# Exponentials and sums first in the next attention slot, and the low halves of the expert weights on DVE instead of POOL

## The chip, the core and the metric

The kernel runs on one core of a Trainium2 chip. The metric is the device time of one launch in microseconds (us). Five engines work side by side, each through its own list of instructions in the order in which they are written: TensorE (PE), VectorE (DVE), ScalarE (ACT), GpSimd (POOL) and SyncE (SP), which here only issues DMAs. They meet through semaphores: `then_inc` counts one up when an instruction has finished, `wait_ge` holds an engine until a count is reached. A wait holds back everything behind it on its engine.

## The reference, cut to what matters

Token selection, one attention layer with quantized values, and a mixture of experts. The part that the change touches first is the softmax in whole numbers, once per batch and head:

```python
x_int = x / scale
x_int = x_int - jnp.max(x_int, axis=-1, keepdims=True)
x_int = jnp.maximum(x_int, n * x0_int)
q = jnp.floor(x_int / x0_int)
r = x_int - x0_int * q
z = r * (r + b_int) + c_int
exp_int = jnp.maximum(jnp.floor(z * jnp.exp2(n - q)), 0.0)
exp_sum = jnp.sum(exp_int, axis=-1, keepdims=True)
ratio = jnp.round(exp_sum / jnp.maximum(exp_int, 1.0))
# out = a power of two that the ratio picks
```

The experts' weights w1 (16 x 192 x 384) and w2 (16 x 192 x 192) meet activations of which the reference takes 32-bit products:

```python
h = jnp.einsum('th,ehf->tef', t, w1) + b1
h = _swiglu(h)
y = jnp.einsum('tei,eih->teh', h, w2) + b2
```

## The kernel before, in words

**Stages.** From 0 to about 74 us tokens are ranked and gathered. From 74 to about 410 us runs attention; from about 429 to 620 us the experts' steps; then the sums are put together. The change lies in the attention.

**Slots.** The 32 batches of 88 tokens are packed in 8 quads of 4 batches, a quad in 3 tiles of 128 rows, which gives 24 tiles. Attention is a software pipeline: `slot(st, n, q)` is written once for each engine, and slot `st` does the softmax of tile `st` and, beside it, work of tiles before and after it. `i = st % 3` is the place in the quad `q = st // 3`. What each engine does in a slot, and in which order, is the order of the calls in its `slot`; nothing is planned at run time.

**The softmax in a slot.** PE makes scores, ACT turns them into whole numbers `S_u` (L934). DVE: maximum `negmx` (L1422), `S_w` (L1427). ACT: the quotient `S_g` (L1011). DVE: remainder `S_rho` (L1461) and the power of two `S_pow` (L1464). ACT: `S_sq`, the square (L1039). DVE: the exponentials `S_e` (L1497) and their sums `esum` (L1501). ACT: an inverse root of `S_e` (L1051) and its square (L1057), both written into `S_sq`; together they are 1/e, called y below. In the next slot DVE makes `S_ratio` (L1446), `S_rb` (L1451) and `S_p` (L1455). SP transposes `S_p` by DMA into `pTs` (`turn_p`, L547), PE multiplies it with the values (`pO`, L1856).

**What else shares the slots.** ACT and PE make the next quad's queries and keys through one PSUM bank `pX`: `project_qk` on PE (L1710), `quant_qk` on ACT (L926). In the slot with i = 0 the chunk 0 comes last, in the one with i = 1 the chunk 5; on PE both stand behind the `pO` matmuls, so behind the transposed `S_p`. Rows of a quad finished two quads ago go to the router: `high_rows` (ACT, i = 0), `low_tail` (DVE, i = 1, L342 and L343), then SP transposes them (`turn_by_load`, L523) ahead of this slot's `S_p`, PE makes the router's logits (`gate_rows`, L1780) and DVE picks four experts per row (`top_experts`, L1350 to L1362). That is in slots 7, 10, 13, 16, 19 and 22, called gate slots below. POOL casts, and sends rows with indirect DMAs (L765).

**Expert weights.** SP loads them in pairs of experts in two staging buffers. A weight is kept as two 16-bit numbers, high and low. ACT scales the pair in place (`scale_pair`, L903 and L905, in the slot with i = 2) and rounds it to the high half (`split_pair`, L912, in the next slot with i = 0, ahead of `S_sq`). POOL subtracts: `low_pair` (L664), 4 instructions per pair, in the slot with i = 0. SP's load of the pair after next waits for these (`stage_low`).

Of the kernel before, what the change touches and what calls it, by code (L numbers as in the profile page):

```python
# [62 lines left out]
def audio_tower(nc, x, tok_w, tok_b, w_qkv, b_qkv, w_proj, b_proj, sw_qkv, sw_proj, s_a1, s_attn,  # L63
                s_a2, s_a3, ffn_scale, gate_w, gate_b, w1, b1, w2, b2, out):
    ctx = ExitStack()
    with ctx:
# [600 lines left out]

# [181 lines left out]
        def _(act):  # L849
# [48 lines left out]
            def scale_pair(m):  # L898

                st, two = stage_in[m % 2], bass.ds(2 * m, 2)  # L900
                act.wait_ge(stage_loaded[m % 2], 16 * 12 * (m // 2 + 1))
                for h in range(2):
                    act.activation(st[:, :, 384 * h:384 * h + 384], st[:, :, 384 * h:384 * h + 384], ACT.Identity,  # L903
                                   scale=fs[:, h:h + 1]).then_inc(s["stage_scaled"], 1)
                act.activation(st[:, :, 768:1152], st[:, :, 768:1152], ACT.Copy, scale=WS).then_inc(s["stage_scaled"], 1)  # L905

            def split_pair(m):

                st, two = stage_in[m % 2], bass.ds(2 * m, 2)
                act.wait_ge(s["stage_scaled"], m * 3 + 3)  # L910
# [1078 lines left out]
```

## Time and profile before

| | us |
|---|---|
| three runs | 658.2, 658.9, 655.73; median 658.2 |
| the profiled execution, its own time | 656.87 |
| its span, first to last instruction | 655.1 |
| DVE busy in the span | 535.2 |
| ACT busy | 443.7 |
| POOL busy | 402.9 |
| PE busy | 369.4 |

The span is 1.77 us shorter than the execution's own time. The shares of busy time are means over stages with different limits, so the attention stage has to be read by itself: by DVE's list in order of time with the idle time before each instruction, and by the chain of waits.

### The profile page before, as it was taken

The numbers are of one execution on the slowest core, as the hardware profiler recorded it, in microseconds if no ns is written. First come the engines' busy times: TensorE is split into PE (matmuls) and PEld (weight loads), VectorE is DVE, ScalarE is ACT, GpSimd is POOL, SyncE is SP. The second block draws the span as 40 slices with busy tenths as digits, with TensorE's granted clock in tenths as the row PEclk, the third lists the DMA queues.
The fourth block names the chain that finished last, engine by engine and source line by source line (L and its number), as shares of the span: only waits on it lengthen the run. The fifth ranks groups of instructions, "written<-read, shape, count | busy, mean of one in ns | idle before, by whom it ended". The sixth has DMA issues, their size and how long they took to land.

```text
span 655.1 us, 13415 instructions
## 1 busy us (share of the span) xinstructions
PE 369.4 (56%) x3593; PEld 236.0 (36%) x3593; DVE 535.2 (82%) x1380; ACT 443.7 (68%) x782; POOL 402.9 (62%) x450
## 2 busy tenths in 40 slices
PE   0598254072452633534536221278979999999264
PEld 0144112031130311312313111256757777777153
DVE  3688699679898897798998989669769998988566
ACT  0046657478767677677686765376878899998753
POOL 9773433431546487586785885477777777777600
PEclk9999555555555555555555555578989999999679
DMA  8546997786959969743422432466467776682098
GB/s 196 67 64 179 366 279 154 257 250 209 304 124 335 226 205 324 154 102 85 114 53 61 101 73 64 107 147 135 116 142 141 124 136 137 137 143 60 14 390 306
DMA packets 191976, 107.76 MB, mean 164 GB/s; under 512 B 137746, under 2 KB 186011, under 8 KB 191906
## 3 DMA queue, kind: packets, MB, share of 16 engines
q1 hardware_dynamic: 181634, 89.22, 56.2%
q0 software_dynamic: 10272, 17.70, 8.8%
q8 instruction: 33, 0.54, 0.4%
q14 instruction: 37, 0.30, 0.2%
HBM read 23.61 MB, written 60.67 MB: 129 GB/s over the span
## 4 chain that ended last, share of the span: by engine, by line
PE 27%; DVE 23%; SPq 13%; issue 13%; DMA 12%; ACT 8%; POOL 2%; DVEq 0%; POOLq 0%; ACTq 0%
PE pS L1925 8%; DMA pTs<-S_p 5%; PE pP L1925 5%; SPq L523 5%; PE pX L1943 4%; DVE S_e L1497 3%; DVE negmx L1422 3%; PE pO L1943 3%; SPq L611 2%; DMA w2s<-expert_rows 2%; SPq L514 2%; PE pS L1666 2%; DMA arena<-in_x_dram 2%; PE pS L1668 2%; DMA bias_rows_hl<-bias_hl 2%
## 5 line engine op out<-in xcount | busy, mean ns | idle before, releaser
L836 POOL DMA_INDIRECT expert_rows<-stage,dest x118 | 124.0, 1051 | 37.3 <-issue 29.6
L765 POOL DMA_INDIRECT region<-rows,slots x60 | 73.7, 1228 | 23.5 <-issue 16.3
L758 POOL CAST arena<-arena 128x384 bf16<-128x384 int8 x42 | 27.0, 643 | 70.0 <-ACT arena L926 69.3
L1843 PE MATMUL pP<-WpT,oq 128*128 128x192 bf16 x72 | 15.9, 359 | 74.0 <-ACT oq L1025 69.2
L1710 PE MATMUL pX<-arena,WA 128*128 128x384 f16 x86 | 34.9, 509 | 39.1 <-ACT arena L926 28.2
L765 POOL DMA_INDIRECT region<-arena,slots x36 | 45.5, 1265 | 18.4 <-issue 11.2
L926 ACT ACTIVATE arena<-pX,qkB,qkA 128x384 int8<-128x384 f32 x43 | 28.4, 661 | 41.6 <-PE pX L1710 41.6
L664 POOL TENSOR_TENSOR w1s<-stage,w1s 128x768 f16<-128x768 f32 (+1 forms) x16 | 33.8, 2113 | 32.9 <-ACT w2s L912 32.3
L1856 PE MATMUL pO<-pTs,vq 88*32 88x96 bf16 (+1 forms) x576 | 12.5, 238 | 71.5 <-DMA pTs<-S_p 71.3
L1497 DVE SCALAR_TENSOR_TENSOR S_e<-S_sq,kf,S_pow 128x1056 f32<-128x1056 f32 x24 | 38.2, 1591 | 16.7 <-ACT S_sq L1039 16.6
L1011 ACT ACTIVATE S_g<-S_w,kf 128x1056 int16<-128x1056 uint16 x24 | 30.3, 1264 | 27.7 <-DVE S_w L1427 27.7
L1051 ACT ACTIVATE S_sq<-S_e,kf 128x1056 f32<-128x1056 f32 x24 | 28.1, 1171 | 26.0 <-DVE S_e L1497 25.7
L1628 DVE TENSOR_SCALAR arena<-pS 128x512 f32<-128x512 f32 x59 | 40.4, 685 | 4.8 <-PE pS L1925 3.6
L1446 DVE SCALAR_TENSOR_TENSOR S_ratio<-esum,S_sq 128x1056 uint16<-128x1056 f32 x24 | 30.9, 1287 | 9.8 <-ACT S_sq L1057 9.8
L1856 PEld LDWEIGHTS pO<-pTs,vq 88*32 88x32 bf16 x576 | 8.6, 118 | 80.7 <-DMA pTs<-S_p 80.4
L1737 PE MATMUL pS<-arena 32*96 32x88 bf16 (+1 forms) x576 | 33.3, 280 | 5.7 <-ACT S_u L934 4.7
L1843 PEld LDWEIGHTS pP<-WpT,oq 128*128 128x128 bf16 x72 | 7.8, 130 | 78.5 <-ACT oq L1025 71.5
L1943 PE MATMUL pX<-w2s,stage 128*128 x264 | 32.6, 250 | 3.8 <-ACT stage L1086 3.0
L1925 PE MATMUL pS<-arena,w1s 128*128 128x256 f16 x224 | 34.0, 283 | 0.0
L1422 DVE TENSOR_REDUCE negmx<-S_u 128x12 f32<-128x1056 int8 x24 | 29.8, 1243 | 4.7 <-ACT S_u L934 4.7
L1461 DVE SCALAR_TENSOR_TENSOR S_rho<-S_g,kf,S_w 128x1056 int16<-128x1056 int16 x24 | 32.6, 1358 | 1.3 <-ACT S_g L1011 1.3
L1427 DVE SCALAR_TENSOR_TENSOR S_w<-S_u,kf,negmx 128x1056 uint16<-128x1056 int8 x24 | 32.4, 1349 | 0.8
(428 smaller groups left out, 1434.6 us busy)
## 6 DMA issues: line engine op xcount, KB each, us to landing
region<-zrow SPq DMA_DIRECT2D x11, 3200.0 KB, 12.2
w1s<-expert_rows SPq DMA_DIRECT2D x16, 384.0 KB, 8.0
stage<-in_L_ffn_w_dram SPq DMA_DIRECT2D x16, 192.0 KB
stage<-in_L_ffn_w_dram SPq DMA_DIRECT2D x32, 96.0 KB
w2s<-expert_rows SPq DMA_DIRECT2D x8, 384.0 KB, 11.7
arena<-in_x_dram SPq DMA_DIRECT2D x4, 672.0 KB
expert_rows<-stage,dest POOLq DMA_INDIRECT x118
out_dram<-xsel SPq DMA_DIRECT2D x8, 198.0 KB
```

Source lines behind the costliest of these rows:

```text
L523: sp.dma_start(xTr[:, :, 128 * i:128 * i + 128], rows[q % 3][:, i, 0:2 * C], transpose=True).then_inc(s["turned"], 16)
L664: pool.tensor_tensor(ws[rows, kind + 1, two, :], st[rows, :, at:at + width], ws[rows, kind, two, :], ALU.subtract).then_inc(s["stage_low"], 1)
L765: pool.indirect_dma_start(region_rows, bass.IndirectOffsetOnAxis(ap=slots[q % 3][:, i, m:m + 1], axis=0), rows[q % 3][:, i, :].bitcast(I16 ...
L836: pool.indirect_dma_start(y_dram, bass.IndirectOffsetOnAxis(ap=dest[(st - 7) % 8][:, j:j + 1], axis=0), ysb[b][:, j, :], None, bounds_chec ...
L1422: dve.tensor_reduce(negmx[:, :], S_u[:, :, :], AX, ALU.max, negate=True).then_inc(s["max_ready"], 1)
L1461: dve.scalar_tensor_tensor(S_rho[:, :, :], S_g[:, :, :], k(K_X), S_w[:, :, :], ALU.mult, ALU.subtract).then_inc(s["rho_ready"], 1)
L1497: dve.scalar_tensor_tensor(S_e[:, :, :], S_sq[:, :, :], k(K_KK), S_pow[:, :, :].bitcast(BF16), ALU.add, ALU.mult).then_inc(s["e_ready"], 1)
L1628: dve.tensor_scalar(lin[r], hidLC[r], -6.0 * XS * WS, 8.0 * XS * WS, ALU.max, ALU.min).then_inc(s["l_done"], 1)
L1710: ins = pe.matmul(bank[:, 0:384], W[:, 128 * c:128 * c + 128], xT[:, kind, :], start=n == 0, stop=n == 2)
L1737: ins = pe.matmul(pS[rows, j, KEEP * c:KEEP * c + width], qT[r][blk, c, at:at + m], keys, start=True, stop=True)
L1925: ins = pe.matmul(dst, w1s[:, kind, bass.ds(k_, 1), 128 * window:128 * window + 128].rearrange("p o f -> p (o f)"), rhs, start=n == 0, sto ...
L1943: ins = pe.matmul(y_ps(st - 5)[:, j, :], lhs, w2s[:, kind, bass.ds(k_, 1), :].rearrange("p o f -> p (o f)"), start=n == 0, stop=n == 4)
```

## The change

1. `S_e` and `esum` leave the end of slot `st` and come at the beginning of slot `st + 1` on DVE: `S_e`, then the choice of experts of the slot before if that was a gate slot, then `negmx`, then `esum`, then `S_w`.
2. The inverse root and the square that make y leave the end of ACT's slot and come first in the next one. They are written into a new buffer `S_y`, so `S_sq` holds only the square of the remainder.
3. ACT no longer scales a weight pair in place: `high_pair` writes the high half with the scale in the same pass, 3 instructions instead of 5, in the slot with i = 2 behind `S_sq`. For pair 0 it comes behind the first `S_u` instead of ahead of it.
4. `low_pair` goes from POOL to DVE: 4 instructions per pair that scale and subtract in one pass, in the slot with i = 0 behind `S_pow`.

```diff
@@ POOL @@
-            def low_pair(m):
-                pool.wait_ge(s["stage_high"], m * 2 + 2)
...
-                    pool.tensor_tensor(ws[rows, kind + 1, two, :], st[rows, :, at:at + width], ws[rows, kind, two, :],
-                                       ALU.subtract).then_inc(s["stage_low"], 1)
-                if i == 0 and st < NT:
-                    low_pair(q)
@@ ACT @@
+            def high_pair(m):
                 act.wait_ge(stage_loaded[m % 2], 16 * 12 * (m // 2 + 1))
                 for h in range(2):
+                    act.activation(w1s[:, 2 * h, two, :], st[:, :, 384 * h:384 * h + 384], ACT.Identity,
+                                   scale=fs[:, h:h + 1]).then_inc(s["stage_high"], 1)
+                act.activation(w2s[:, 0:4:2, two, :].rearrange("p k e f -> p e k f"),
+                               st[:, :, 768:1152].rearrange("p e (k f) -> p e k f", k=2),
+                               ACT.Copy, scale=WS).then_inc(s["stage_high"], 1)
...
-            scale_pair(0)
             quant_scores(0)
-            split_pair(0)
+            high_pair(0)
...
+                if 1 <= st <= NT:
+                    act.wait_ge(s["e_ready"], n)
...
+                    act.activation(S_y[:, :, :], S_e[:, :, :], ACT.Abs_reciprocal_sqrt,
+                                   bias=k(K_TINY)).then_inc(s["inv_root"], 1)
+                    act.wait_ge(s["inv_root"], n)
+                    act.activation(S_y[:, :, :], S_y[:, :, :], ACT.Square).then_inc(s["y_ready"], 1)
...
-                if i == 2 and st <= 20:
-                    scale_pair(q + 1)
-                if i == 0 and 3 <= st < NT:
-                    split_pair(q)
...
                     act.activation(S_sq[:, :, :], S_rho[:, :, :], ACT.Square, bias=k(K_NB2)).then_inc(s["sq_ready"], 1)
+                if i == 2 and st <= 20:
+                    high_pair(q + 1)
@@ DVE @@
+                if 1 <= st <= NT:
+                    dve.wait_ge(s["sq_ready"], n)
+                    dve.wait_ge(s["pow_ready"], n)
...
+                    dve.scalar_tensor_tensor(S_e[:, :, :], S_sq[:, :, :], k(K_KK), S_pow[:, :, :].bitcast(BF16), ALU.add,
+                                             ALU.mult).then_inc(s["e_ready"], 1)
+                if 0 < st <= NT and quad_at(st - 1, GATE) is not None:
+                    top_experts(quad_at(st - 1, GATE))
                 if st < NT:
...
                     dve.tensor_reduce(negmx[:, :], S_u[:, :, :], AX, ALU.max, negate=True).then_inc(s["max_ready"], 1)
+                if 1 <= st <= NT:
+                    dve.wait_ge(s["e_ready"], n)
+                    dve.wait_ge(s["ratio_ready"], n - 1)
+                    dve.tensor_reduce(esum[:, :], S_e[:, :, :], AX, ALU.add).then_inc(s["sum_ready"], 1)
...
+                if i == 0 and st < NT:
+                    low_pair(q)
...
+            def low_pair(m):
+                dve.wait_ge(s["stage_high"], m * 3 + 3)
+                for rows, kind, ws, at, width, scale in (
+                        (slice(0, 128), 0, w1s, 0, 2 * FF, fs[:, 0:1]), (slice(0, CB), 2, w1s, 384, 2 * FF, fs[0:CB, 1:2]),
+                        (slice(0, 128), 0, w2s, 768, C, WS), (slice(0, CB), 2, w2s, 960, C, WS)):
+                    dve.scalar_tensor_tensor(ws[rows, kind + 1, two, :], st[rows, :, at:at + width], scale,
+                                             ws[rows, kind, two, :], ALU.mult, ALU.subtract).then_inc(s["stage_low"], 1)
```

Three places in the order of the instructions. The first is DVE's list at the end of gate slot 10 and the start of slot 11, before; `arena`, `best`, `keep`, `keyv`, `early` belong to `top_experts`.

```order
L1497 SCALAR_TENSOR_TENSOR S_e<-S_sq,kf,S_pow 128x1056
L1501 TENSOR_REDUCE esum<-S_e 128x12
L1350 COPY arena<-pX 128x48
L1353 MAX best<-arena 128x8 x3
L1355 COPY keep<-best 128x3x4
L1357 MATCH_REPLACE keyv<-keep,arena 128x16 x3
L1360 SCALAR_TENSOR_TENSOR early<-keyv,valid 128x48
L1362 TENSOR_TENSOR arena<-arena,best 128x48
L1422 TENSOR_REDUCE negmx<-S_u 128x12
L1427 SCALAR_TENSOR_TENSOR S_w<-S_u,kf,negmx 128x1056
L1435 TENSOR_TENSOR pr<-pP,pA 128x192
```

The same place on DVE after the change (`S_e` here is L1401, `top_experts` L1326 to L1338, `negmx` L1408, `esum` L1412):

```order
L1401 SCALAR_TENSOR_TENSOR S_e<-S_sq,kf,S_pow 128x1056
L1326 COPY arena<-pX 128x48
L1329 MAX best<-arena 128x8 x3
L1331 COPY keep<-best 128x3x4
L1333 MATCH_REPLACE keyv<-keep,arena 128x16 x3
L1336 SCALAR_TENSOR_TENSOR early<-keyv,valid 128x48
L1338 TENSOR_TENSOR arena<-arena,best 128x48
L1408 TENSOR_REDUCE negmx<-S_u 128x12
L1412 TENSOR_REDUCE esum<-S_e 128x12
L1418 SCALAR_TENSOR_TENSOR S_w<-S_u,kf,negmx 128x1056
L1426 TENSOR_TENSOR pr<-pP,pA 128x192
```

`S_e` stays ahead of `top_experts`, which waits for PE; `esum` moved from ahead of `top_experts` to behind `negmx`.

The second is ACT's list from the last score conversion in slot 0 on, before. `arena<-pX` is `quant_qk` of chunk 0, ACT_TABLE_LOAD brings in the table of the inverse root.

```order
L1039 ACTIVATE S_sq<-S_rho,kf 128x1056
L1051 ACT_TABLE_LOAD
L1051 ACTIVATE S_sq<-S_e,kf 128x1056
L926 ACTIVATE arena<-pX,qkB,qkA 128x384
L1057 ACTIVATE S_sq<-S_sq 128x1056
L1011 ACTIVATE S_g<-S_w,kf 128x1056
```

The same place after the change:

```order
L1021 ACTIVATE S_sq<-S_rho,kf 128x1056
L905 ACTIVATE arena<-pX,qkB,qkA 128x384
L989 ACT_TABLE_LOAD
L989 ACTIVATE S_y<-S_e,kf 128x1056
L992 ACTIVATE S_y<-S_y 128x1056
L997 ACTIVATE S_g<-S_w,kf 128x1056
```

The table load and the inverse root stood ahead of `quant_qk`, and stand behind it now.

The third is ACT's list from the last `S_sq` (slot 23) on, before; `arena<-arena 128x48 x6` are the routers' exponentials (`exp_gates`, L968).

```order
L1039 ACTIVATE S_sq<-S_rho,kf 128x1056
L1051 ACTIVATE S_sq<-S_e,kf 128x1056
L1057 ACTIVATE S_sq<-S_sq 128x1056
L962 ACTIVATE rs<-rs 128x3
L968 ACT_TABLE_LOAD
L968 ACTIVATE arena<-arena 128x48 x6
```

The same place after the change:

```order
L1021 ACTIVATE S_sq<-S_rho,kf 128x1056
L941 ACTIVATE rs<-rs 128x3
L947 ACT_TABLE_LOAD
L947 ACTIVATE arena<-arena 128x48 x6
L989 ACT_TABLE_LOAD
L989 ACTIVATE S_y<-S_e,kf 128x1056
L992 ACTIVATE S_y<-S_y 128x1056
```

The exponentials with their table load stood behind y; they stand ahead of it now, and a second table load has come between.

## Rows read from the trace of the kernel before

**Rows 1.** Page, part 1: busy us, share of the span, instructions

```profile
PE 369.4 (56%) x3593; PEld 236.0 (36%) x3593; DVE 535.2 (82%) x1380; ACT 443.7 (68%) x782; POOL 402.9 (62%) x450
```

**Rows 2.** Busy time by stretch: stretch, length, PE, PEld, DVE, ACT, POOL, clock

```profile
271.00:313.00 42.00, 18.64 (x226) 9.77 (x226) 38.28 (x71) 30.66 (x40) 31.69 (x28) 0.50 0.42 100
```

**Rows 3.** Chain that ended last, gate slot 16: start us, length us, engine, tile, line

```profile
300.70 1.18 SPq L523
...
304.57 5.52 DMA pTs<-S_p
```

**Rows 4.** DVE in order of time, slots 15 and 16: start, length, [idle before <-releaser]

```profile
293.24 2.18 DVE L1497 SCALAR_TENSOR_TENSOR S_e<-S_sq,kf,S_pow 128x1056 f32<-128x1056 f32 x1 [1.07 <-ACT S_sq L1039]
295.45 1.25 DVE L1501 TENSOR_REDUCE esum<-S_e 128x12 f32<-128x1056 f32 x1
296.62 1.24 DVE L1422 TENSOR_REDUCE negmx<-S_u 128x12 f32<-128x1056 int8 x1
297.90 1.32 DVE L1427 SCALAR_TENSOR_TENSOR S_w<-S_u,kf,negmx 128x1056 uint16<-128x1056 int8 x1
...
299.40 0.80 DVE L342 TENSOR_TENSOR arena<-tn,arena 128x192 f16<-128x192 f32 x1
...
311.19 0.21 DVE L1350 COPY arena<-pX 128x48 f32<-128x48 f32 x1 [1.77 <-PE pX L1780]
```

**Rows 5.** ACT in order of time, slots 0 and 1

```profile
81.06 1.28 ACT L1051 ACT_TABLE_LOAD   x1
...
85.88 0.67 ACT L926 ACTIVATE arena<-pX,qkB,qkA 128x384 int8<-128x384 f32 x1 [1.16 <-PE pX L1710]
86.45 1.07 ACT L1057 ACTIVATE S_sq<-S_sq 128x1056 f32<-128x1056 f32 x1
```

**Rows 6.** Chain that ended last, slots 1 to 3

```profile
87.55 1.27 DVE S_ratio L1446
...
89.78 2.65 SPq L547
...
95.37 2.45 SPq L480
...
113.79 9.99 DMA bias_rows_hl<-bias_hl
```

**Rows 7.** ACT in order of time, slot 4

```profile
131.88 0.67 ACT L926 ACTIVATE arena<-pX,qkB,qkA 128x384 int8<-128x384 f32 x1 [7.14 <-PE pX L1710]
```

**Rows 8.** DVE in order of time, slots 4, 5 and 6

```profile
133.56 1.26 DVE L1446 SCALAR_TENSOR_TENSOR S_ratio<-esum,S_sq 128x1056 uint16<-128x1056 f32 x1 [5.95 <-ACT S_sq L1057]
...
153.08 1.32 DVE L1497 SCALAR_TENSOR_TENSOR S_e<-S_sq,kf,S_pow 128x1056 f32<-128x1056 f32 x1 [0.65 <-ACT S_sq L1039]
...
164.76 1.73 DVE L1497 SCALAR_TENSOR_TENSOR S_e<-S_sq,kf,S_pow 128x1056 f32<-128x1056 f32 x1 [1.23 <-ACT S_sq L1039]
```

**Rows 9.** POOL in order of time, slot 15

```profile
286.10 1.43 POOL L765 DMA_INDIRECT region<-rows,slots  x1 [0.31 <-issue]
...
292.63 4.28 POOL L664 TENSOR_TENSOR w1s<-stage,w1s 128x768 f16<-128x768 f32 x2
```

**Rows 10.** DVE in order of time, slots 15 and 24

```profile
286.87 1.25 DVE L1446 SCALAR_TENSOR_TENSOR S_ratio<-esum,S_sq 128x1056 uint16<-128x1056 f32 x1
...
291.36 0.41 DVE L1471 SCALAR_TENSOR_TENSOR xsel<-pr,sc,xsel 128x192 f32<-128x192 int8 x1
...
411.75 0.36 DVE L342 TENSOR_TENSOR arena<-tn,arena 128x192 f16<-128x192 f32 x1 [1.62 <-ACT arena L947]
```

**Rows 11.** ACT in order of time, slots 23 and 24

```profile
404.06 1.18 ACT L1051 ACTIVATE S_sq<-S_e,kf 128x1056 f32<-128x1056 f32 x1 [2.46 <-DVE S_e L1497]
...
406.47 1.28 ACT L968 ACT_TABLE_LOAD   x1
407.76 0.91 ACT L968 ACTIVATE arena<-arena 128x48 f32<-128x48 f32 x6
```

**Rows 12.** SP's queue in order of time, gate slot 7

```profile
171.77 5.83 SPq L523 DMA_TRANSPOSE early<-arena  x3
```

More of the change, by code:

```diff
@@ L135, in audio_tower @@
         S_e = sb("S_e", [128, H, KEEP], F32)
+        S_y = sb("S_y", [128, H, KEEP], F32)
         S_ratio = sb("S_ratio", [128, H, KEEP], U16)
@@ L902, in scale_pair @@
                 for h in range(2):
[L903 to L910, printed above, removed]
-                for ws, at, width in ((w1s, 0, 2 * FF), (w2s, 768, C)):
-                    act.activation(ws[:, 0:4:2, two, :].rearrange("p k e f -> p e k f"),
-                                   st[:, :, at:at + 2 * width].rearrange("p e (k f) -> p e k f", k=2),
-                                   ACT.Copy).then_inc(s["stage_high"], 1)
+                    act.activation(w1s[:, 2 * h, two, :], st[:, :, 384 * h:384 * h + 384], ACT.Identity,
[3 more added lines that the diff above has]
+                               ACT.Copy, scale=WS).then_inc(s["stage_high"], 1)
             def high_x(q):
@@ L1047, in slot @@
                     quant_qk(q + 1, 4, fill(st, "qk", 4))
-                if st < NT:
-                    act.wait_ge(s["e_ready"], n + 1)
-                    act.activation(S_sq[:, :, :], S_e[:, :, :], ACT.Abs_reciprocal_sqrt,
-                                   bias=k(K_TINY)).then_inc(s["inv_root"], 1)
                 if nxt and i < 2:
                     quant_qk(q + 1, 5 * i, fill(st, "qk", 5 * i))
-                if st < NT:
-                    act.wait_ge(s["inv_root"], n + 1)
-                    act.activation(S_sq[:, :, :], S_sq[:, :, :], ACT.Square).then_inc(s["y_ready"], 1)
                 if quad_at(st, COEFFS) is not None:
@@ L1490, in slot @@
                     route_constants()
-                if st < NT:
-                    dve.wait_ge(s["sq_ready"], n + 1)
-                    dve.wait_ge(s["pow_ready"], n + 1)
-                    dve.wait_ge(s["inv_root"], n)
-                    dve.wait_ge(s["sum_ready"], n)
-                    dve.scalar_tensor_tensor(S_e[:, :, :], S_sq[:, :, :], k(K_KK), S_pow[:, :, :].bitcast(BF16), ALU.add,
-                                             ALU.mult).then_inc(s["e_ready"], 1)
-                    dve.wait_ge(s["e_ready"], n + 1)
-                    dve.wait_ge(s["ratio_ready"], n)
-                    dve.tensor_reduce(esum[:, :], S_e[:, :, :], AX, ALU.add).then_inc(s["sum_ready"], 1)
-                if quad_at(st, GATE) is not None:
+                if quad_at(st, GATE) is not None and st >= NT:
                     top_experts(quad_at(st, GATE))
@@ L1507, in slot @@
                     step_table(0)
+            def low_pair(m):
+                st, two = stage_in[m % 2], bass.ds(2 * m, 2)
+                dve.wait_ge(s["stage_high"], m * 3 + 3)
[4 more added lines that the diff above has]
+                                             ws[rows, kind, two, :], ALU.mult, ALU.subtract).then_inc(s["stage_low"], 1)
             def step_blocks(late):
```

19 lines of the change are left out of this document (8 added, 11 removed).

## The prediction

> **What bounds the kernel now.** I read the busy shares first, then the same by stretch, then the chain of waits, and last each engine's list in order of time. The page has DVE at 82% of the span and nobody near it [rows 1]. In one quad of the attention, 42 us long, DVE works 38.3 us, ACT 30.7, POOL 31.7 and PE 18.6, at a granted clock of 0.50 [rows 2]. So DVE is the bound of the attention wherever it doesn't wait, and about 4 us of the 42 are its waits.
>
> Where these lie, the chain shows. In a gate slot it leaves DVE at `low_tail`, runs through SP's three row transposes and the transpose of `S_p` (issued at 304.57, landed 5.52 us later) and comes back to DVE at `top_experts`, which idled 1.77 us for it [rows 3, 4]. From `top_experts` through slots i = 2 and i = 0 to the next `low_tail` DVE is on the path without a break but one: in the slot with i = 0 `S_e` waits for `S_sq`, which ACT starts only behind the two instructions of `split_pair` [rows 4]. So a quad is a DVE stretch and a transpose stretch, and what is added to DVE outside of the gate slot's second half is paid. Before slot 5 it is otherwise: there the chain runs over SP, from the first `S_p` over the weight loads and the bias's DMA (9.99 us) to the third `S_p` [rows 6], and DVE idles 5.95 us in slot 4 [rows 8].
>
> **The low halves on DVE.** Eight pairs, 4 instructions each. No row shows this instruction at this size. Its kind (two tensors, one scalar) takes 1.32 us for 1056 elements (`S_w`, and the wait behind it ends 1.23 us after its start) and 0.41 us for 192 [rows 4, 10]: about 1.05 ns per element and 0.2 us. That makes 768 elements 0.94 us and 384 elements 0.54 us from start to start; 2 x 0.94 + 2 x 0.54 = 3.0 us per pair. From below: half of it, 1.5, if 16-bit results let it run at twice the rate; `S_w` with 8-bit input and 16-bit output doesn't. From above: what POOL's work does to `S_e` (2.18 for the 1.32 that it takes alone), 4.9 us. I take 3.0, since both rows are of this kind.
>
> Pairs 0 and 1 (slots 0 and 3) lie ahead of the 5.95 us idle and cost nothing; without that idle they would cost 4 to 5 us. The other six (slots 6, 9, 12, 15, 18, 21) cost 6 x 3.0 = 17.8 us of DVE, against which stands:
> - the wait of `S_e` for `S_sq`: with `split_pair` gone from ahead of it `S_sq` is done before DVE has made the low halves. 1.23 us in two slots, 1.07 in three, 1.06 in one [rows 8, 4]: 6.7 us.
> - `S_e` itself: POOL's `low_pair` (2 x 2.14 us from 292.63 on) ran beside it [rows 9]. It took 1.73 in slots 6, 9 and 21 and 2.2 in 12, 15 and 18 [rows 8, 4], 1.32 alone: 3.9 us.
> - the first instruction of `low_tail`: 0.80 with POOL's subtraction beside it, 0.36 without [rows 4, 10], six times: 2.6 us.
>
> 17.8 - 6.7 - 3.9 - 2.6 = +4.6 us. Without the relief from POOL it would be +11.1. In slot 5 `S_e` waited 0.65 us behind `scale_pair` [rows 8]; `high_pair` stands behind `S_sq`: -0.65.
>
> The Trainium skill, "SBUF — State Buffer", section "SBUF: two separate sides", says that a POOL instruction and a DVE instruction with two SBUF inputs exclude each other, and that the later one stands still for the whole of the other. The trace agrees for POOL's subtraction in kind. It speaks against this change, since the new DVE instructions have two such inputs and POOL sends rows in these slots; by it they could stand behind each send. But `S_ratio`, with two inputs too, took its usual 1.25 us at 286.87 beside a send that ran from 286.10 to 287.53 [rows 9, 10]. By the rule alone each send met would cost up to its own length; by the row, nothing.
>
> **The order on DVE.** `S_e` was already directly ahead of the next slot's `negmx`, so in 13 of the 19 changes of slot from 5 to 23 only `negmx` and `esum` swap. Before, `esum` waited for `S_e`'s end (2.21 us after its start at a length of 2.18), followed by `negmx` after 1.17 and by `S_w`, waiting for `negmx`, after 1.28 [rows 4]. Now each has an independent one ahead of it, and starts about 0.1 before the end of the last: 0.11 + 0.11 = 0.22 less. 13 x 0.22 = -2.9 us. From below nothing, from above 3.
>
> In the six gate slots `esum` stood ahead of the wait for PE, inside the idle time; now it comes behind `top_experts`, in the stretch that is paid. It adds 1.17, less 0.11 for the closer start of `S_w`: 6 x 1.06 = +6.4 us. What is late next is nothing new: the gate comes from SP and the DMA, which don't wait for `esum`. Together +3.5 us.
>
> **The order on ACT.** In a gate slot y comes about 1.1 us later after `quant_qk` (the inverse root now follows it), so `S_ratio` and `S_p` may too; SP is busy with three transposes from `low_tail` on (3.8 us at the least), and `S_p` is ready in time. That costs nothing there. Two places have no such cover.
>
> Slot 1: ACT waited for PE's chunk 0 until 85.88, then needed 1.07 us for the square, and `S_ratio` began at 87.55 [rows 5, 6]. The table load (1.28) and the inverse root (1.18) were over by then. Now they come behind that `quant_qk`, as the order shows: `S_ratio`, `S_p` and SP's transpose come 2.5 us later. The earlier first `S_u` (2.5 us of scaling gone from ahead of it) gains nothing, since ACT waits for the same DMA. The SP chain then runs to slot 4. Some of its issues are long (2.45 us for one load) [rows 6], which I read as a queue that is full until earlier fills are through, and such a delay is absorbed in part. Ends 0 and 2.5, I take 1.5. In slot 4 `quant_qk` comes 7.14 us late and DVE stands waiting for y [rows 7, 8]; the inverse root now comes behind it: +1.1.
>
> Slots 23 and 24: the routers' exponentials come ahead of y. ACT idled 2.46 us before the last inverse root; into it go the small root (0.19), a table load (1.28), the exponentials (0.91) and the load back (1.28) [rows 11]: 3.7 us, and the small root first waits some 0.6 us for DVE. 3.7 + 0.6 - 2.46 = +1.8, of which I take 1.7; the chain goes from this y to the last `S_p` and on to the experts. The Trainium skill, "ScalarE: Activation LUTs", section "What ACT_TABLE_LOAD costs", puts a switch of tables at about 2.66 us, a drain with it; the row has 1.28 with the next instruction 0.01 behind it, so the trace shows no drain here. By the page three switches stand 1.4 longer, and the sum would be 4 us higher.
>
> POOL's 8 x 7.1 us of subtraction go, which frees no path: POOL's casts wait for ACT.
>
> **Sum.** +1.5 (slot 1) + 1.1 (slot 4) - 0.65 (slot 5) + 4.6 (low halves) + 3.5 (order on DVE) + 1.7 (end) = +11.8 us. The execution took 656.87 us, its span 655.1: 656.87 + 11.8 = 668.6. The median of the runs is 1.3 above that execution. I say 669.
>
> **Rivals.**
> A. The delays are absorbed. SP's transposes at 171.77 took 5.83 us instead of the 3.8 of slot 16, so in the early gate slots something else ends them [rows 12], and a later `low_tail` would cost less; slot 1's delay vanishes too, and the new instructions cost 2.5 per pair. Then 11.8 - 1.5 - 2 x 1.5 - 2.5 = +4.8: 662. Against: the late gate slots have no such wait.
> B. Faster than before. The place is the transpose stretch of the gate slots. POOL's subtraction ended at 300 there, its casts and sends came behind it, and `S_p` needed 5.1 to 5.6 us to land in three of them, 3.7 to 3.9 in the others. If POOL, idle earlier, spreads its sends away from the transposes, and SP's issues fall to 3.8 (2.0 less in slot 7, more in 10 and 13) as well, each gate slot gains. Price: 3 x 1.7 + 7.5 = 12.6 us, 656.9 + 11.8 - 12.6 = 656, and with slot 1's delay absorbed 654.5. It decides from 2.0 us per gate slot on. Against: the sends of these slots are tied to ACT's `quant_qk` by their place in POOL's list, not to `low_pair`.
> C. The new instructions on DVE meet POOL's sends and run like `S_e` beside POOL's subtraction: 4.9 per pair, +11.4: 680.
> D. Each switch of tables drains: +4: 673.
>
> **Chances.** The forecast's own case 0.57 (664 to 673), A 0.17, B 0.08, C 0.08, D 0.10. What this kernel's measurement can tell from no change is 0.5%, 3.3 us, so faster is below 654.9 and slower above 661.5. Faster: most of B, 0.07. Same: the rest of B, half of A and a little of the forecast's low end, 0.12. Slower 0.81. The range goes from the lower part of A to between D and C: 659 to 677.
>
> **What would show it.** Right: `low_pair` at about 1.0, 1.0, 0.6 and 0.6 us; `S_e` without a wait for `S_sq` in the slots with i = 0, and near 1.32 there; 1.1 us more from `top_experts` to `S_w`; slot 1's `S_ratio` at 90; the last inverse root at about 1.7 us after its `S_e`; the experts' stage as long as before. Wrong: a pair under 2 us on DVE; gate slots in which `S_p` lands in under 4 us throughout; or a quad shorter than 42 us.

## The result: 669.15 us, 1.75% slower

| | before | after |
|---|---|---|
| median of the runs, us | 657.42 (655.73 to 658.9, 4 runs) | 669.15 (666.86 to 671.02, 4 runs) |
| the profiled execution: its time / its span, us | 656.87 / 655.1 | 671.02 / 669.1 |

The ratio is 1.0175, with a 95% interval of 1.0145 to 1.0204: 11.7 us more, where 11.8 was the sum. The profiled execution of after is its slowest; the four spans go from 665.1 to 669.1, so a difference below 1 us at one place can belong to the execution and is leaned on only where several kernels show it.

The page of after, part 1 (busy us, share, instructions), answers to [rows 1]: DVE has 7.4 us more, ACT 13.7 and POOL 60.8 less.

```profile
PE 366.6 (55%) x3593; PEld 233.9 (35%) x3593; DVE 542.6 (81%) x1412; ACT 430.0 (64%) x766; POOL 342.1 (51%) x418
```

The same by stretch, from one reading of the gate to the next (slots 13 to 16), answers to [rows 2]. The quad takes 43.38 us; between the same two readings it took 42.10 before.

```profile
275.99:319.37 43.38, 18.60 (x226) 9.77 (x226) 39.02 (x75) 29.08 (x37) 22.64 (x24) 0.50 0.45 96
```

DVE in order of time, slots 15 and 16 (start, length, idle before it), answers to [rows 4, 8]:

```profile
298.53 1.93 DVE L1498 SCALAR_TENSOR_TENSOR w1s<-stage,fs,w1s 128x768 f16<-128x768 f32 x2
300.39 1.01 DVE L1498 SCALAR_TENSOR_TENSOR w2s<-stage,w2s 128x384 f16<-128x384 f32 x2
301.33 0.14 DVE L1300 TENSOR_TENSOR newton<-rs 128x3 f32<-128x3 f32 x1
...
302.70 1.30 DVE L1401 SCALAR_TENSOR_TENSOR S_e<-S_sq,kf,S_pow 128x1056 f32<-128x1056 f32 x1
303.92 1.25 DVE L1408 TENSOR_REDUCE negmx<-S_u 128x12 f32<-128x1056 int8 x1
305.08 1.25 DVE L1412 TENSOR_REDUCE esum<-S_e 128x12 f32<-128x1056 f32 x1
306.24 1.31 DVE L1418 SCALAR_TENSOR_TENSOR S_w<-S_u,kf,negmx 128x1056 uint16<-128x1056 int8 x1
...
307.73 0.35 DVE L343 TENSOR_TENSOR arena<-tn,arena 128x192 f16<-128x192 f32 x1
...
319.37 0.21 DVE L1326 COPY arena<-pX 128x48 f32<-128x48 f32 x1 [3.02 <-PE pX L1772]
```

The reader is to see four things. The low halves take 2.80 us from their start to the next instruction. `S_e` follows without a wait and takes 1.30 us, not 2.18. From the start of `S_e` to `S_w` there are 3.54 us, not 4.66: 0.88 of that is `S_e` itself, 0.24 the new order. And DVE idles 3.02 us for the gate, not 1.77, since `esum` is no longer inside that idle.

The chain that ended last, gate slot 16, answers to [rows 3]. Its shape is the old one:

```profile
308.58 1.18 SPq L524
...
312.46 5.80 DMA pTs<-S_p
```

ACT at slot 1 and at the end of the attention answers to [rows 5, 11]:

```profile
88.07 0.67 ACT L905 ACTIVATE arena<-pX,qkB,qkA 128x384 int8<-128x384 f32 x1 [8.33 <-PE pX L1702]
88.75 1.28 ACT L989 ACT_TABLE_LOAD   x1
90.05 1.17 ACT L989 ACTIVATE S_y<-S_e,kf 128x1056 f32<-128x1056 f32 x1
...
413.53 1.28 ACT L947 ACT_TABLE_LOAD   x1
414.83 0.91 ACT L947 ACTIVATE arena<-arena 128x48 f32<-128x48 f32 x6
415.75 1.28 ACT L989 ACT_TABLE_LOAD   x1
417.04 1.17 ACT L989 ACTIVATE S_y<-S_e,kf 128x1056 f32<-128x1056 f32 x1
```

**Where the time went.** Starts of the same instruction in both profiles, after less before:

| place | shift, us |
|---|---|
| ACT's `quant_qk` of slot 1 (85.88, 88.07) | +2.2 |
| DVE's `S_ratio` of slot 1 (87.55, 92.37) | +4.8 |
| DVE's `S_ratio` of slot 4 (133.56, 138.59) | +5.0 |
| gate of slot 7 (182.51, 187.75) | +5.2 |
| gate of slot 10 (224.01, 230.65) | +6.6 |
| gate of slot 13 (269.09, 275.99) | +6.9 |
| gate of slot 16 (311.19, 319.37) | +8.2 |
| gate of slot 19 (353.39, 362.60) | +9.2 |
| gate of slot 22 (392.59, 402.81) | +10.2 |
| last `S_e` (402.71, 413.97) | +11.3 |
| last `S_ratio` (406.39, 419.36) | +13.0 |
| end of the span | +14.0 |

The first 2.2 us are put down to the execution and not to the change: 1.1 us of them are there before any instruction that was changed (the same copy on DVE, L1350 before and L1326 after, starts at 58.38 and 59.45), and SP's fills began 1.6 us later (63.49 for 61.91). In the kernels below, this `quant_qk` starts between 84.5 and 87.8 (e5's 88.8 apart, where it stands behind y), in no order that follows what was changed in them. The last 1.0 us lie behind the last `S_ratio`, where the kernels below need between 247.6 and 250.5 us for work that is the same in all (before 248.7, after 249.7). So the two profiles show 10.8 us between the two ends, where the sum has 11.8: 2.8 by slot 4's `S_ratio` (priced 2.6) and 8.0 from there to the last one (priced 9.2).

### The profile page after: what moved, and what is told of

Its sections match the earlier page's. It is cut to its first block, busy times and chain, and to the rows that moved or that the text cites. A ratio compares the mean times of both kernels' runs of the same rounds, so it can differ in the third digit from the quotient of the medians.

```text
span 669.1 us, 13415 instructions
## 1 busy us (share of the span) xinstructions
PE 366.6 (55%) x3593; PEld 233.9 (35%) x3593; DVE 542.6 (81%) x1412; ACT 430.0 (64%) x766; POOL 342.1 (51%) x418
## 4 chain that ended last, share of the span: by engine, by line
DVE 27%; PE 23%; issue 14%; SPq 13%; DMA 12%; POOL 5%; ACT 5%; POOLq 0%; DVEq 0%; ACTq 0%
PE pS L1917 6%; DMA pTs<-S_p 6%; SPq L524 4%; POOL expert_rows L822 4%; PE pP L1917 4%; DVE esum L1412 3%; DVE S_rho L1452 3%; PE pX L1935 3%; PE pO L1935 3%; DVE S_ratio L1437 2%; SPq L612 2%; SPq L515 2%; DMA w2s<-expert_rows 2%; DMA arena<-in_x_dram 2%; DVE w1s L1498 2%
## 5 line engine op out<-in xcount | busy, mean ns | idle before, releaser
L746 POOL CAST arena<-arena 128x384 bf16<-128x384 int8 x42 | 23.5, 560 | 161.6 <-ACT arena L905 161.3
L753 POOL DMA_INDIRECT region<-rows,slots x60 | 75.6, 1260 | 32.7 <-issue 16.9
L753 POOL DMA_INDIRECT region<-arena,slots x36 | 45.3, 1260 | 21.5 <-issue 11.8
L1437 DVE SCALAR_TENSOR_TENSOR S_ratio<-esum,S_y 128x1056 uint16<-128x1056 f32 x24 | 30.0, 1250 | 20.3 <-ACT S_y L992 20.3
L1401 DVE SCALAR_TENSOR_TENSOR S_e<-S_sq,kf,S_pow 128x1056 f32<-128x1056 f32 x24 | 31.7, 1319 | 9.0 <-ACT S_sq L1021 8.9
L1021 ACT ACTIVATE S_sq<-S_rho,kf 128x1056 f32<-128x1056 int16 x24 | 28.1, 1171 | 15.3 <-DVE S_rho L1452 15.3
L1452 DVE SCALAR_TENSOR_TENSOR S_rho<-S_g,kf,S_w 128x1056 int16<-128x1056 int16 x24 | 36.2, 1507 | 1.3 <-ACT S_g L997 1.3
L1917 PE MATMUL pS<-tEb,w1s 128*128 128x256 f16 x118 | 32.5, 276 | 0.0
L989 ACT ACTIVATE S_y<-S_e,kf 128x1056 f32<-128x1056 f32 x24 | 28.0, 1167 | 6.5 <-DVE S_e L1401 6.5
L1408 DVE TENSOR_REDUCE negmx<-S_u 128x12 f32<-128x1056 int8 x24 | 29.9, 1245 | 2.4 <-ACT S_u L913 2.4
```

Source lines behind the costliest of these rows:

```text
L753: pool.indirect_dma_start(region_rows, bass.IndirectOffsetOnAxis(ap=slots[q % 3][:, i, m:m + 1], axis=0), rows[q % 3][:, i, :].bitcast(I16 ...
L1401: dve.scalar_tensor_tensor(S_e[:, :, :], S_sq[:, :, :], k(K_KK), S_pow[:, :, :].bitcast(BF16), ALU.add, ALU.mult).then_inc(s["e_ready"], 1)
L1408: dve.tensor_reduce(negmx[:, :], S_u[:, :, :], AX, ALU.max, negate=True).then_inc(s["max_ready"], 1)
L1437: dve.scalar_tensor_tensor(S_ratio[:, :, :], esum[:, :].unsqueeze(2).broadcast_to([128, H, KEEP]), 2.0 ** -MOST, S_y[:, :, :], ALU.max, AL ...
L1452: dve.scalar_tensor_tensor(S_rho[:, :, :], S_g[:, :, :], k(K_X), S_w[:, :, :], ALU.mult, ALU.subtract).then_inc(s["rho_ready"], 1)
L1917: ins = pe.matmul(dst, w1s[:, kind, bass.ds(k_, 1), 128 * window:128 * window + 128].rearrange("p o f -> p (o f)"), rhs, start=n == 0, sto ...
```

## Experiments

Four kernels each ran on one chip, beside the kernel before, whose median was 657.32 (e1 to e4), 657.68 (e5 to e8) and 657.83 (e9 to e12), over the runs up to then. The intervals are 0.2 to 0.4% wide to each side, so a difference between two medians of this table is known to 2 or 3 us.

| run | median, us | ratio to before (95%) |
|---|---|---|
| e1 weights only | 661.62 | 1.0055 (1.0025 to 1.0085) |
| e2 order only | 663.03 | 1.008 (1.005 to 1.011) |
| e3 low halves twice | 678.87 | 1.0324 (1.0293 to 1.0354) |
| e4 esum ahead | 662.79 | 1.007 (1.0046 to 1.0095) |
| e5 y first | 659.02 | 1.0028 (1.0009 to 1.0048) |
| e6 fill later | 669.19 | 1.0169 (1.0125 to 1.0213) |
| e7 fill later, low twice | 678.94 | 1.0324 (1.0282 to 1.0366) |
| e8 square first | 655.47 | 0.9967 (0.9949 to 0.9985) |
| e9 send later | 665.33 | 1.01 (1.0071 to 1.0128) |
| e10 before, send later | 654.71 | 0.9945 (0.9924 to 0.9967) |
| e11 combined | 658.09 | 1.0015 (0.9992 to 1.0039) |
| e12 combined, send later | 652.65 | 0.9917 (0.989 to 0.9943) |

**The two halves of the change.** e1 is the kernel before with the weights' part alone (`high_pair` behind `S_sq`, `low_pair` on DVE), e2 with the order alone (`S_e`, `negmx`, `esum` and `S_y`; the weights as before).

> The kernel before with the expert weights alone as in the change: three instructions on ACT behind S_sq, the low halves on DVE behind S_pow in the slots with i = 0; exponentials, sums and y stay where they were. Theory (ledger): low halves +4.6 us (17.8 of new DVE work, less 6.7 of waits for S_sq, 3.9 and 2.6 of relief from POOL), slot 5 -0.65: +4.0 us on the 657.4 of before, 661.4. S_e near 1.32 us without a wait in slots 6, 9, 12, 15, 18, 21. Rival (the waits and POOL's relief pay for the new work): 655 to 658. Rival (the low halves are slowed on DVE by POOL's sends): 668 or more.

> The changed order of exponentials, sums and y alone; the expert weights as in the kernel before (scaling and rounding on ACT ahead of S_sq, subtraction on POOL). Theory: order on DVE +3.5, slot 1 about +1.5, slot 4 +1.1, the end +1.7: +7.8 us, 665.2. Rival (the order costs nothing, all of the loss is the low halves on DVE): 657 to 659.

Measured +4.3 and +5.7, together 10.0 of the 11.7. The weights' part agrees with the priced 4.0, by the medians. The profiles put less of it at its place. The stretch that the low halves lengthen, from `S_w` of a slot with i = 0 to the end of `low_tail` in the next slot, grew by 0.3 to 0.9 us in the six quads of e1, 3.3 us in all. From e2 to the kernel after, which differ in the weights alone, the same six stretches grew by 3.9. The price was 4.6. From slot 1's `quant_qk` to the last `S_ratio` e1 took 2.9 us more than before, 1.0 of it ahead of slot 4's `S_ratio`, where nothing was priced; 1.8 lie behind the last `S_ratio`, in the scatter named above.

The order's part is 2.2 short of 665.2. In its profile `S_p` landed in slots 13 and 16 in 4.5 and 4.4 us, where it had been 5.1 and 5.5, and in slot 19 in 5.9 for 5.6: 1.4 us that had no term. From slot 1's `quant_qk` to `S_ratio` it took 4.31 us, as in after (4.30), where it had been 1.67: the delay of 2.6 (2.5 in the prediction). From that `quant_qk` to slot 4's `S_ratio` it took 2.4 us longer than before, in after 2.8; slots 1 and 4 were priced at 2.6.

**What the low halves cost.** e3 has each pair's four instructions in the kernel after a second time:

```diff
+                for turn in range(2):
+                    if turn:
+                        dve.wait_ge(s["stage_scaled"], m * 4 + 4)
+                    low_once(st, two, s["stage_low" if turn else "stage_scaled"])
+
+            def low_once(st, two, done):
+
                 for rows, kind, ws, at, width, scale in (
...
```

> The changed kernel with the four low-half instructions of each pair done twice, the second time over the first with the same values. Theory: DVE is the bound in the slots with i = 0, so each of six pairs adds its 3.1 us again, the pairs of slots 0 and 3 lie ahead of an idle time of 6 us and add nothing: +18 to +19 us on 669, 687 to 688. Rival (waits absorb work on DVE, since transposes end them at a time of their own): +10 us or less, below 680.

A miss: +9.7 us, not +18, in the range of the rival. Against after, the gates of slots 7, 10 and 13 were -1.2, -0.2 and +0.2 us, those of slots 16, 19 and 22 +3.4, +6.4 and +9.3. So the three late pairs pay 3.1 us each, in full, and in the three early ones 1.9 to 2.5 of 2.9 us were given back by the time of the gate. SP's queue in gate slot 10 (start, length; x3 are `low_tail`'s transposes), first after, then e3, seems to say why:

```profile
207.18 5.82 SPq L548 DMA_TRANSPOSE pTs<-S_p  x1
213.04 1.10 SPq L500 DMA_DIRECT2D region<-zrow  x1
218.70 6.60 SPq L524 DMA_TRANSPOSE early<-rows  x3
225.40 1.42 SPq L548 DMA_TRANSPOSE pTs<-S_p  x1
```

```profile
211.97 0.95 SPq L500 DMA_DIRECT2D region<-zrow  x1
220.38 4.67 SPq L524 DMA_TRANSPOSE early<-rows  x3
225.15 1.52 SPq L548 DMA_TRANSPOSE pTs<-S_p  x1
```

The row transposes start 1.7 us later and end 0.25 earlier. My theory was that they stand behind the fill of 3.2 MB that SP issues in slots 6, 9 and 12. e6 (after) and e7 (e3) issue those three fills a slot later:

```diff
-                if i != 1 and 2 + 2 * q + i // 2 < REGION // STEP:
+                if (i == 2 or i == 0 and q < 2 or i == 1 and q >= 2) and 2 + 2 * q + i // 2 < REGION // STEP:
                     fill_share(2 + 2 * q + i // 2)
```

> The kernel after, with the three fills of 3.2 MB that SP issues in slots 6, 9 and 12 (any of them that exist there) issued one slot later, behind the transpose of S_p and ahead of the weight loads. Theory (the fill's backlog is what stretches the three row transposes to 5.8 to 7.2 us in slots 7, 10 and 13): these transposes fall to about 3.8 us, and the gates of these slots come about 2 us earlier; the fill then meets the next S_p transpose and the weight loads, which may give some of it back: 663 to 669. Rival (something else, the weights' loads or POOL's sends, stretches them): they stay at 6 us, and the time stays at 669 or grows by what the moved fill costs.

> The same move of the fills in the kernel that makes the low halves twice (each pair's four instructions are issued a second time, with the same result). To be read against the run with the fills moved alone. Theory (the backlog absorbed the early pairs): without it all six pairs cost their 3.1 us, so the distance is 6 x 3.0 = 18 us instead of the 9.7 measured with the fills in their place. Rival (the early pairs are absorbed by something else): it stays at 9 to 11 us.

Half of the theory held. The fills do stretch the row transposes: in e6 the three of gate slot 10 took 4.46 us instead of 6.60, those of slot 7 3.78 instead of 6.20. But neither time moved (669.19, 678.94), and e7's distance to e6 stayed at 9.7. The chain of e6 in gate slot 10 names a second cover, which ends at the same time:

```profile
206.64 9.44 DMA pTs<-S_p
216.08 0.04 issue
216.13 0.52 PE pO L1848 x24
216.65 1.09 PE pX L1702 x3
...
224.99 1.15 PE pX L1702 x3
...
229.59 0.56 PE pX L1772 x15
230.15 0.02 issue
230.18 0.22 DVE arena L1326
```

The transpose of slot 9's `S_p` (e7: 10.63 us) lands behind the fill of slot 8, and everything up to the gate hangs on it: PE's chunks, ACT's `quant_qk`, PE again. Neither SP's transposes nor DVE's low halves are on that path. So two covers of about the same height are what I read as absorbing the early pairs. For the first, e6 shows that the fills make it; that they make the second too is read from this chain and not shown, since no kernel without them was run.

**What esum costs.** In e4 `esum` stands ahead of `top_experts` in the slots behind a gate, in the kernel after:

```diff
-                if 0 < st <= NT and quad_at(st - 1, GATE) is not None:
+                gated = 0 < st <= NT and quad_at(st - 1, GATE) is not None
+                if gated:
+                    dve.wait_ge(s["e_ready"], n)
+                    dve.wait_ge(s["ratio_ready"], n - 1)
+                    dve.tensor_reduce(esum[:, :], S_e[:, :, :], AX, ALU.add).then_inc(s["sum_ready"], 1)
+                if gated:
                     top_experts(quad_at(st - 1, GATE))
...
-                if 1 <= st <= NT:
+                if 1 <= st <= NT and not gated:
```

> The changed kernel with esum ahead of the choice of experts in the six slots behind a gate slot, as before; everywhere else it stays behind negmx. Theory: esum goes back into DVE's idle time (1.3 to 3.0 us there), 6 x 1.06: -6.4 us, 662.8; in the first two gate slots that idle time is only 1.3 and 1.4 us, still enough. Rival (the gate is not what ends the gate slot, esum's place is no matter): 669.

669.15 to 662.79 is -6.4, the priced 6 x 1.06, but the two profiles tell it less neatly. Of the six gates, `S_w` behind each starts another 1.04 us earlier against after (at slot 8 -1.85, with the gate at -0.81). Of that, 1.5 are lost again by the gate of slot 13 and some 0.9 at three others, so that `S_w` of slot 23 has won 3.8 since the gate of slot 7; 0.7 lie ahead of slot 1, and 0.9 behind the last `S_ratio`. So the term is shown in size at its place six times, and its survival to the end only in part; the median's agreement has some luck in it. A small part of the gain is another one: `S_rho` of slots 11, 14 and 17, longer in after (see below), was back at 1.30 us, which is worth 0.15 us in each.

**What y's place costs.** In e5 `quant_qk` of chunks 0 and 5 and the routers' exponentials stand behind the next slot's y, in the kernel after.

```diff
                     act.activation(S_y[:, :, :], S_y[:, :, :], ACT.Square).then_inc(s["y_ready"], 1)
+                    if st == NT:
+                        for e in range(TAILQ):
+                            exp_gates(e)
+                    pi, pq = (st - 1) % 3, (st - 1) // 3
+                    if pq + 1 < NQ and pi < 2:
+                        quant_qk(pq + 1, 5 * pi, fill(st - 1, "qk", 5 * pi))
...
-                if nxt and i < 2:
-                    quant_qk(q + 1, 5 * i, fill(st, "qk", 5 * i))
...
-                if st == NT - 1:
-                    for e in range(TAILQ):
-                        exp_gates(e)
```

> The kernel after, with y taken ahead of the other work again at the two places of the prediction's ACT terms: quant_qk of chunks 0 and 5 stands behind the next slot's y, and the routers' exponentials stand behind the last y. Both moves are in one kernel because their places lie 300 us apart and the profile separates them. If the terms were right, S_ratio of slot 1 starts 2.5 us earlier (near 90), S_ratio of slot 4 gains the 1.1 us of the inverse root, and the last S_ratio starts 1.7 us after its S_e's square instead of waiting 2.5 us; the net of slot 1 and 4 is 1.6 us as the order alone showed, the end 1.7: in all 3.3 us, 665.9. Rival: S_ratio is early in all gate slots as well, which frees nothing (SP busy) or, if S_p was late there in part, gives up to 1 us each: 660. Other rival: quant_qk now comes later, PE and SP wait for it, and 1 us per quad is lost: 673.

-10.1 us, three times what the terms gave, and near the 660 of the first rival. Up to slot 6 it gained 1.0 us beyond its earlier start (`S_w` of slot 6 1.8 us sooner, of slot 0 0.75), and at the last `S_ratio` 1.7, as priced. From the gate of slot 7 to that of slot 22 it gained 4.5 more, in the gate slots, in the chain's step from SP's issue to the landing of `S_p`. Gate slot 19, after and then e5:

```profile
355.84 5.66 DMA pTs<-S_p
```

```profile
351.38 3.73 DMA pTs<-S_p
```

In slots 13, 16 and 19 this step takes 5.5, 5.8 and 5.7 us in after, 3.8, 4.5 and 3.7 in e5. POOL's rows in slot 19 show one send just behind the issue in after (at +0.56 us), which in e5 is at +0.81:

```profile
356.40 0.98 POOL L753 DMA_INDIRECT region<-arena,slots  x1 [0.22 <-issue]
```

```profile
352.19 0.98 POOL L753 DMA_INDIRECT region<-arena,slots  x1 [0.16 <-issue]
```

e9 (after) and e10 (before) move that send alone:

```diff
-                            if 1 <= c <= 3:
+                            if c in (1, 4, 5):
                                 send(1)
```

> The kernel after, with one thing changed on POOL: in a slot with i = 1 the second of its two sends stands behind the cast of chunk 4 instead of chunk 2, some 2 to 4 us later, away from SP's transposes. Why: in the slots 13, 16 and 19 the S_p transpose landed 5.5, 5.8 and 5.7 us after its issue with a send 0.6 to 0.8 us behind the issue, while with y taken first it landed in 3.8, 4.5 and 3.7, and the kernel ran 10 us shorter where the prediction's terms gave 3.3. Theory (the send next to the transpose holds it up): it lands in 3.8 us in all three, -1.7 - 2.0 - 1.9 = -5.6 us, 663.6. Rival (the landing hangs on something else that moved with y, or the send holds up whatever it meets): under 1.5 us of change, 668 to 670.

> The same move of the second send in the kernel before. There the landings were 5.1, 5.5 and 5.6 us in slots 13, 16 and 19. Theory: 3.8 in each, -1.3 - 1.7 - 1.8 = -4.8 us from 657.7, 652.9; this would be the saving that the prediction's rival B spoke of, reached by the sends and not by the subtraction. Rival (POOL's subtraction, not the send, holds the S_p transpose here): no change, 657 to 658.

-3.8 and -3.1 us, two thirds of what was expected. In slot 19 the landing fell to 4.0 and 3.9 us, in slot 13 to 4.6 and 4.4, but in slot 16 it stayed at 5.2 and 5.5, with the send 4.7 to 5.3 us behind the issue. The shorter landings are where the time came from: from the gate of slot 7 to that of slot 22, e9 gained 3.6 us on after, and its landings of slots 10 to 19 are 3.7 us shorter; in e10 it is 2.4 and 2.5. So the place of the send is a cause, and not the only one; what holds slot 16's transpose stays open. In e9 it took SP 2.54 us to issue it, in e10 1.45.

Nor is a send close behind the issue enough. Before and e2 have it 0.45 us behind in slot 16; it took 5.52 us before, and in e2

```profile
307.06 4.36 DMA pTs<-S_p
```

In slot 22 there is a send about 0.75 us behind the issue before, in after, in e5 and in e9, and the landing took 3.9 us in all of them. After:

```profile
397.85 3.86 DMA pTs<-S_p
```

```profile
398.59 0.97 POOL L753 DMA_INDIRECT region<-rows,slots  x1 [0.30 <-issue]
```

What else must come together with the send was not found.

**The square first.** e8 is the kernel before with `scale_pair` and `split_pair` behind `S_sq`.

> The kernel before, with scale_pair and split_pair moved behind S_sq in their slots on ACT and nothing else changed. The prediction priced S_e's wait for S_sq behind split_pair at 6.7 us in six slots, and 0.65 in slot 5. If both are on the path and ACT has the room afterwards: 657.3 - 7 = 650. If POOL's subtraction, which then starts about 1 us later, meets low_tail or the sends instead, half of it comes back: 654. If the early slots (6, 9, 12) are absorbed by the transposes' backlog as in the twice-made low halves, 3.3 us are left of the gain: 653.5.

-2.2 us of 7. `S_w` behind the waits started 1.7 us sooner (slot 10: -2.45 against before, where the gate of slot 7 had -0.71), and by the next gate nothing of it was left (-0.77, then -0.75 and -0.85). POOL's subtraction, set free later, now ran beside other instructions of DVE. Slot 10:

```profile
207.25 2.43 DVE L1427 SCALAR_TENSOR_TENSOR S_w<-S_u,kf,negmx 128x1056 uint16<-128x1056 int8 x1
...
210.58 1.26 DVE L343 TENSOR_TENSOR rows<-tn,rows 128x384 f16<-128x384 f32 x1
```

Before, these took 1.32 and 0.55 us; the 1.1 and 0.7 eat the gain, six times: from `S_w` of a slot with i = 0 to the end of `low_tail`, the six stretches are 0.2 us shorter in all. The wait was real, but taking it away gave next to nothing there as long as POOL's subtraction stayed. Of the 2.2 us, the profile has 0.7 by the gate of slot 7 and 0.5 in the landing of slot 19; the rest isn't assigned.

**The parts together.** e11 keeps the new order, makes the low halves on POOL, and has e8's, e4's and e5's edits; e12 has e9's as well.

> A candidate from the measured parts: the change's new order of S_e, negmx and esum and its separate S_y are kept; the weights are scaled and split on ACT, but behind S_sq, and their low halves are made on POOL as before; esum stands ahead of the experts' reading in the slots behind a gate; quant_qk of chunks 0 and 5 and the routers' exponentials stand behind y. By the sum of the runs: 663.0 (order alone) - 6.4 (esum) - 5 to 8 (y first; the 10.1 us measured on the kernel after, less what the order alone had already absorbed) - 2.2 (square first) = 647 to 649. Rival (each of the parts gained the same S_p landings, so they don't add): 652 to 654.

> The candidate with the second send behind the cast of chunk 4 as well. If y first had already taken the send away from the transpose, nothing is left to gain: within 1.5 us of the candidate. If the candidate's S_p transposes in slots 13, 16 and 19 still take over 5 us, up to 5 us less: 643.

e11 is a miss by 10 us: no faster than before, and 4 us above its rival too. Two things are seen in its profile. The first is e8's collision, which the sum had entered as a gain. In slot 16 of e11, where after has 1.31 and 0.56:

```profile
295.70 2.67 DVE L1449 SCALAR_TENSOR_TENSOR S_w<-S_u,kf,negmx 128x1056 uint16<-128x1056 int8 x1
...
299.29 1.26 DVE L344 TENSOR_TENSOR arena<-tn,arena 128x384 f16<-128x384 f32 x1
```

The order alone had already brought `S_e` beside POOL's subtraction from 2.2 to 1.7 us in slots 12, 15 and 18. On top of it, "square first" made the six stretches from `S_w` to the end of `low_tail` 2.4 us longer than in e2 (15.10 for 14.66 us in slot 16), where 2.2 us of gain had been counted.

The second is in the gate slots. Against before the gates of slots 7, 10 and 13 came at -0.3, +0.1 and +0.3. SP's row transposes there had stretched again, in slot 13 to 8.0 us in three pieces:

```profile
255.22 2.48 SPq L524
257.74 2.82 SPq L524
260.60 2.69 SPq L524
263.34 0.02 SPq L547
263.38 4.92 DMA pTs<-S_p
```

That a part of the 6.4 and 10.1 us had been gained above this cover and could not be gained again below it is my reading, and not shown. In slot 19 the landing was 5.5 us again, with the send 0.45 us behind the issue. e12 moves the send, lands `S_p` in 4.1, 4.1 and 3.8 us in slots 13, 16 and 19, and takes 652.65: 5.4 less than e11, 5.2 less than the kernel before (0.8%) and 16.5 less than the kernel after. It beats both. So the collision (2.4 and the 2.2 counted) and the place of the send (5.4) are together as large as the miss.

## Why the prediction was right, point by point

- **Sum, +11.8.** Measured 11.7 in the medians; at their places the terms come to 10.8 in the two profiles. That the medians agree to 0.1 us is luck: their interval alone is 2 us to each side, and the 669 was reached from an execution of 656.87 us, with the median of before then at 658.2 and later at 657.42.
- **Low halves, +4.6.** Right in kind, about 1 us too much in size: 3.3 us in e1 and 3.9 from e2 to after, at their place. The four instructions took 1.00, 1.00, 0.54 and 0.54 us, 2.80 us per pair from the first to what follows, where 3.0 was priced. The three savings came as told: no wait of `S_e` in the slots with i = 0, `S_e` at 1.30 us, `low_tail`'s first row at 0.35. In e2 the order alone brought `S_e` in slots 12, 15 and 18 from 2.2 to 1.7 us, so 1.4 of the 3.9 us counted for `S_e` came with the order too, and are not gained twice. What the prediction didn't see is that only late pairs pay a further microsecond in full (e3).

```profile
L1498 DVE SCALAR_TENSOR_TENSOR w1s<-stage,fs,w1s x16: 999/1004/1015, 78.8 to 384.8; 128x768 f16<-128x768 f32 x8, 64x768 f16<-64x768 f32 x8
L1498 DVE SCALAR_TENSOR_TENSOR w2s<-stage,w2s x16: 539/540/543, 80.7 to 386.2; 128x384 f16<-128x384 f32 x8, 64x384 f16<-64x384 f32 x8
```

- **Order on DVE, +3.5.** From the reading of the gate to `S_w` there are 3.94 us, 2.90 before: +1.04 where 1.06 was priced, and e4 takes it back. The closer starts are there too: from the `S_e` of slot 8, 1.32 us long in both kernels, to the `S_w` of slot 9 there were 3.80 us before and 3.55 after. With the low halves the price was 8.1 us in six quads, 1.35 each; the gates moved by 1.4, 0.3, 1.3, 1.0 and 1.0 from one to the next. The early one that is short, slot 13's, is where e4 lost most: a part is absorbed there. The five steps make 5.0 us for a price of 6.7, so the late part's missing time lies here.
- **Order on ACT, +1.5 and +1.1.** Right. From `quant_qk` of slot 1 to that of slot 4 after has 1.6 us more, and y in slot 4 comes 1.2 later; e2 has 2.4 for both. Behind them less is left: e5 gave back 1.0 by slot 6. `S_ratio` of slot 1 was to start at 90; it did at 92.4, 2.2 of it from ahead of the change.
- **End, +1.7.** Right. The last `S_ratio` was 1.7 us later against its `S_e` in after and in e2, and came back by 1.7 in e5.
- **y in a gate slot, nothing.** Nearly so against before, where the landings of slots 13, 16 and 19 were 5.1, 5.5 and 5.6 us (after 5.5, 5.8, 5.7); but the cover named for it (SP is busy) was not the point. With y first these landings shrink (e5), and some 4 us hung on them beyond the priced 3.3. e9 shows that 3.8 can be had by the send's place alone.
- **The rivals.** A's mechanism exists: it holds in the early gate slots for what comes on top (e3), and slot 13's short step shows some of it for the change itself. Its instructions at 2.5 us do not (and 6 x 0.46 is 2.8, where its sum takes 2.5). B's price of 1.7 us per landing was real in size (e5, e9), and its condition wasn't met by the change, as argued: in slot 19 the send is 0.56 us behind the issue in after, 0.45 before. In e1 one landing was shorter, 4.4 us in slot 16, but the row transposes ahead of it took 1.1 us more. C is false: every pair took 2.8 us, in slot 15 too, where a send of POOL (297.09 to 299.11) still ran when the first instruction began at 298.53. D is false: the table loads took 1.28 us with the next instruction 0.01 to 0.02 us behind, and the Trainium skill's 2.66 us ("ScalarE: Activation LUTs", section "What ACT_TABLE_LOAD costs") is not what these rows show.
- **Not priced.** In slots 11, 14 and 17 `S_rho` took 2.47 us instead of 1.30, and `S_e` in the same slots 1.32 instead of 1.88: the two had swapped which of them meets POOL's low halves of x. e2 shows it, e1 and e4 don't, so it comes from `esum`'s place behind the gate. Other small instructions beside POOL's got shorter by it, so that from `S_w` to the next `S_w` slot 11 takes 13.27 us in after and e2, and 13.12 in e4 and e11, which have the closer starts without the swap: a cost of 0.15 us in each of the three.

## What to carry to other kernels

When work is moved onto the engine that bounds a loop, price what it relieves on that engine as well: here 13.2 of 17.8 us were to come back, and e1's +4.3 us bears that out. Price each edit against the waits that absorb it in its own slot. Don't add savings that were measured one at a time in different kernels: e8's edit, worth 2.2 us in the kernel before, made DVE's list 2.4 us longer in the new order. Look where an engine's order sets the time of another engine's DMA: some 4 us of this kernel hung on when POOL's send meets SP's transpose, not on arithmetic.

## What the runs showed of the hardware

A DVE instruction with two tensors took longer in these runs when one of POOL's subtractions, with two tensors too, ran beside it: `S_e` 2.18 us for 1.30, `S_w` 2.43 (e8) and 2.67 (e11) for 1.32, `S_rho` 2.47 for 1.30. POOL's took longer as well: its two of 768 elements took 4.28 us in slot 15 before, beside `S_e`, and 3.35 in e8, where they start later. After, slot 14: `S_rho` on DVE beside POOL's two subtractions of 0.71 and 0.90 us:

```profile
284.22 2.47 DVE L1452 SCALAR_TENSOR_TENSOR S_rho<-S_g,kf,S_w 128x1056 int16<-128x1056 int16 x1
```

```profile
284.00 0.71 POOL L343 TENSOR_TENSOR arena<-arena 128x192 f16<-128x192 f32 x1
284.67 0.90 POOL L344 TENSOR_TENSOR arena<-arena 128x384 f16<-128x384 f32 x1
```

In e1, with DVE in the old order, the same instruction took 1.30 us:

```profile
277.87 1.30 DVE L1436 SCALAR_TENSOR_TENSOR S_rho<-S_g,kf,S_w 128x1056 int16<-128x1056 int16 x1
```

The transpose of an `S_p` (128 x 12 x 128 numbers of 16 bits, 0.4 MB) took 3.7 to 4.1 us to land in gate slots 7 and 22 of every kernel whose chain shows it. In slots 13, 16 and 19 with a send up to about 0.8 us behind its issue it took from 3.7 (e5) to 6.3 us (e6), 5.5 to 5.8 in after. Behind a fill of 3.2 MB it took 9.4 (e6) and 10.6 us (e7).
